# Denominators of the second attention: sums by TensorE in four column quarters of a bank, in place of GpSimd's additions

## The reference

```python
q = (text_hidden @ Wq).reshape(B, T_text, N_HEADS, HEAD_DIM).transpose(0, 2, 1, 3)
k = (vision_tokens @ Wk).reshape(B, T_vis, N_KV_HEADS, HEAD_DIM).transpose(0, 2, 1, 3)
v = (vision_tokens @ Wv).reshape(B, T_vis, N_KV_HEADS, HEAD_DIM).transpose(0, 2, 1, 3)
scores = jnp.einsum('bhtd,bhsd->bhts', q, k) / scale
scores = jnp.where(mask, scores, -jnp.inf)
attn = jax.nn.softmax(scores, axis=-1)
out = jnp.einsum('bhts,bhsd->bhtd', attn, v)
return out.reshape(B, T_text, N_HEADS * HEAD_DIM) @ Wo
```

## Time and profile before

| what | value |
|---|---|
| median of three runs | 1687.81 us (1685.54 to 1689.53) |
| the profiled execution | 1685.9 us, of it the span 1684.5 us |
| mean granted TensorE clock | 0.942 of 2.4 GHz |
| busy, TensorE matmul | 1454.9 us (86%) |
| busy, VectorE | 1229.2 us (73%) |
| busy, ScalarE | 1127.1 us (67%) |
| busy, GpSimd | 792.1 us (47%) |
| chain that ended last | PE L582 35%, POOL L1878 6%, DVE L1514 3% |

### The profile page before, as it was taken

One profiled execution on the slowest core, in us unless ns is written; L12 is line 12 of the kernel. 1 busy time (PEld: TensorE's weight loads), 2 busy tenths in 40 slices (PEclk: granted clock), 3 DMA queues, 4 the chain that ended last, 5 costly groups with the idle time before them and its releaser, 6 DMA issues.

```text
span 1684.5 us, 25330 instructions
## 1 busy us (share of the span) xinstructions
PE 1454.9 (86%) x8374; PEld 711.7 (42%) x8460; DVE 1229.2 (73%) x2184; ACT 1127.1 (67%) x2020; POOL 792.1 (47%) x615
## 2 busy tenths in 40 slices
PE   5687988888888887688898989899899999999979
PEld 3243343343333343244444444344544455455445
DVE  6765766666686356478887768899589997788937
ACT  3567667667764755477787668678477775788724
POOL 3014013014030001078766749787486877577823
PEclk8798997897999999799999999999999999999989
DMA  4001200200340100100000100000000000000000
GB/s 154 1 1 39 43 1 11 50 1 1 60 176 1 51 1 5 39 21 6 1 1 23 38 20 6 26 1 1 6 26 1 26 1 1 1 1 1 1 1 26
DMA packets 20488, 36.69 MB, mean 22 GB/s; under 512 B 4898, under 2 KB 15238, under 8 KB 19334
## 3 DMA queue, kind: packets, MB, share of 16 engines
q1 hardware_dynamic: 20358, 35.07, 7.2%
HBM read 26.53 MB, written 1.15 MB: 16 GB/s over the span
## 4 chain that ended last, share of the span: by engine, by line
PE 35%; POOL 9%; issue 7%; DVE 5%; ACT 3%; POOLq 0%; DMA 0%; ACTq 0%; DVEq 0%; SPq 0%
PE BK L582 35%; POOL arena L1878 6%; DVE arena L1514 3%; DVE arena L1497 1%; ACT arena L1760 1%; ACT arena L1768 1%; POOL arena L1875 1%; POOL arena L1853 1%; ACT arena L1753 1%; POOL arena L1884 1%; POOL arena L1863 1%; DVE arena L886 0%; PE BK L866 0%; ACT L1753 0%; DVE arena L1528 0%
## 5 line engine op out<-in xcount | busy, mean ns | idle before, releaser
L582 PE MATMUL BK<-arena 128*128 128x512 bf16 (+10 forms) x8044 | 1407.2, 378 | 192.6 <-DVE arena L1497 30.6
L582 PEld LDWEIGHTS BK<-arena 128*128 128x128 bf16 (+7 forms) x8130 | 674.2, 115 | 894.8 <-issue 235.1
L1878 POOL TENSOR_TENSOR arena<-arena 128x512 f32<-128x512 f32 (+1 forms) x352 | 509.5, 1447 | 178.6 <-ACT arena L1753 154.5
L1514 DVE TENSOR_TENSOR arena<-arena 128x512 bf16<-128x512 f32 (+1 forms) x416 | 514.4, 1245 | 39.7 <-ACT arena L1760 38.8
L1753 ACT ACTIVATE arena<-BK,arena 128x512 f32<-128x512 f32 (+1 forms) x416 | 285.9, 687 | 132.3 <-PE BK L582 117.1
L1329 DVE TENSOR_REDUCE arena<-BK 128x1 f32<-128x512 f32 x384 | 244.0, 683 | 65.6 <-PE BK L582 64.4
L1661 ACT ACTIVATE arena<-BK 128x512 f32<-128x512 f32 (+1 forms) x416 | 226.0, 598 | 76.0 <-PE BK L582 69.6
L1760 ACT CAST arena<-arena 128x512 bf16<-128x512 f32 (+1 forms) x416 | 253.3, 609 | 0.0
L1768 ACT ACTIVATE arena<-BK 128x512 bf16<-128x512 f32 (+1 forms) x256 | 130.0, 508 | 87.8 <-PE BK L582 86.7
L1497 DVE CUSTOM_DVE_ANT_0 arena<-BK,arena 128x512 bf16<-128x512 f32 (+1 forms) x256 | 145.7, 569 | 47.4 <-PE BK L582 37.5
L1802 POOL TENSOR_TENSOR arena<-arena 128x256 f32<-128x256 f32 (+6 forms) x45 | 30.2, 671 | 208.1 <-ACT arena L1600 205.7
(11 more groups left out here) (170 smaller groups left out, 863.8 us busy)
## 6 DMA issues: line engine op xcount, KB each, us to landing
arena<-arena SPq DMA_DIRECT2D x144, 50.0 KB, 2.2
arena<-in_ctxT SPq DMA_DIRECT2D x8, 800.5 KB, 4.4
arena<-in_ctxk SPq DMA_DIRECT2D x4, 768.0 KB
arena<-in_wo SPq DMA_DIRECT2D x1, 2048.0 KB, 7.9
arena<-in_wqT SPq DMA_DIRECT2D x1, 2048.0 KB, 7.7
arena<-in_x SPq DMA_DIRECT2D x4, 256.0 KB, 11.0
arena<-in_rsel SPq DMA_DIRECT2D x1, 1024.0 KB, 9.2
arena<-in_rw1T SPq DMA_DIRECT2D x1, 1024.0 KB, 5.1
```

The lines of the kernel that those rows point to most:

```text
L582: return T.matmul(out_, lhsT, rhs, start=start, stop=stop, skip_group_check=True)
L1514: V.tensor_tensor(Pl[k][0:m, :], P1[k][0:m, :], Ph[k][0:m, :], ALU.subtract).then_inc(p_low, 1)
L1878: G.tensor_tensor(acc[0:m, g % 2, :], acc[0:m, g % 2, :], P1[k][0:m, :], ALU.add).then_inc(summed1, 1)
```

## The change

GpSimd no longer adds the exponentials. A new piece `su` follows `v1` after each second tile: TensorE sums a pair of tiles over their keys, with 32 columns of bf16 ones (`onb`) as weights. The high and the low halves of the two tiles go to four different column quarters, rows 0, 32, 64 and 96 of bank 6: four products of 512 columns for each pair, seven `su` pieces to a group, the last of them with one tile and so two products, directly behind the sixth. At the end of the group VectorE takes bank 6 to `den` in one pass of 128 x 512 (`o1a`; rows of a quarter are equal, and a lower bound guards against zero). `o1b` multiplies `den` by `quarter`, a matrix with ones in one row of each quarter, so that bank 7 holds the whole denominators on all partitions, and VectorE inverts all 128 x 512 of them into `rc`. ScalarE's copy, VectorE's two small operations, the four products with one column and GpSimd's diagonals are gone.

What comes with it: `P1` is freed by VectorE's `r1` alone; `Ph` and `Pl` get rings of six (`NH`) and are freed by `su`; `finish` begins two steps earlier in the next group (`kt == 3` in place of 5); `qproj` of stage 2 moves from bank 6 to bank 4, which it shares with `md`; GpSimd sets `quarter` and `least` with eight more small memsets in stage 1.

```diff
-LEAD1, LAG1, NR = 6, 3, 4
+LEAD1, LAG1, NR, NH = 6, 3, 4, 6
+L1SET = 11
...
-    def qproj(self, g, bank=6):
+    def qproj(self, g, bank=4):
...
         def finish(g):
-            piece("o1a", g, bank=7)
+            piece("o1a", g)
             yield
             yield
             piece("o1b", g, bank=7)
...
-            if kt == LAG1 + 2 and s > NKT:
+            if kt == LAG1 and NKT < s < ns:
...
-            if kt > LAG1 + 1:
+            if kt >= LAG1:
                 next(og, None)
...
                 piece("v1", s - LAG1)
+                gv, kv = (s - LAG1) // NKT, (s - LAG1) % NKT
+                if kv and kv % 2 == 0:
+                    piece("su", gv, kv // 2 - 1)
+                    if kv == NKT - 1:
+                        piece("su", gv, kv // 2)
...
-                elif kind == "o1a":
-                    g, = arg
-                    pe.wait_ge(summed1, 12 * (g + 1))
-                    pe.wait_ge(l1_set, 4)
-                    for u in range(4):
-                        t = mm(BK[7][:, u:u + 1], acc[:, g % 2, 128 * u:128 * u + 128], ones[:, 0:1])
-                    t.then_inc(full[7], 1)
+                elif kind == "su":
+                    g, u = arg
+                    if u == 0:
+                        pe.wait_ge(den_taken, g)
+                    for kt in range(2 * u, min(2 * u + 2, NKT)):
+                        k, m = (g * NKT + kt) % NH, rows_of(kt)[0]
+                        for n_, part in enumerate((Ph, Pl)):
+                            at = 64 * (kt % 2) + 32 * n_
+                            t = mm(BK[6][at:at + 32, :], onb[0:m, 0:32], part[k][0:m, :], start=(u == 0), stop=(kt >= 11))
+                    t.then_inc(den_summed, 1)
                 elif kind == "o1b":
                     g, = arg
-                    pe.wait_ge(diag_done, g + 1)
-                    mm(BK[7][:, :], ones[:, :], dg[:, :, :].rearrange("p u n -> p (u n)")).then_inc(full[7], 1)
+                    pe.wait_ge(den_taken, g + 1)
+                    mm(BK[7][:, :], quarter[:, :], den[:, :]).then_inc(full[7], 1)
...
                 elif kind == "o1a":
+                    g, = arg
+                    dve.wait_ge(*summed1(NKT * g + NKT - 1))
+                    dve.wait_ge(l1_set, L1SET)
+                    if g:
+                        dve.wait_ge(*filled("o1b", g - 1))
+                    V.tensor_scalar(den[:, :], BK[6][:, :], least[:, 0:1], None, ALU.max).then_inc(den_taken, 1)
+                elif kind == "o1b":
+                    g, = arg
                     dve.wait_ge(full[7], n + 1)
-                    V.tensor_scalar(dn[:, 0:4], BK[7][:, 0:4], 1e-30, None, ALU.max).then_inc(free[7], 1)
-                    dve.wait_ge(free[7], n + 1)
-                    V.reciprocal(dn[:, 4:8], dn[:, 0:4]).then_inc(dn_recip, 1)
+                    dve.wait_ge(pv_taken, g)
+                    V.reciprocal(rc[:, :], BK[7][:, :]).then_inc(free[7], 1)
...
                     act.wait_ge(p_low, s - NR + 1)
-                    if s >= NR:
-                        go, ko = (s - NR) // NKT, (s - NR) % NKT
-                        act.wait_ge(summed1, 12 * go + max(ko, 1))
...
-                elif kind == "o1b":
-                    g, = arg
-                    act.wait_ge(full[7], n + 1)
-                    act.wait_ge(pv_taken, g)
-                    A.copy(rc[:, :], BK[7][:, :]).then_inc(free[7], 1)
...
-                        G.tensor_tensor(acc[:, g % 2, :], P1[(s - 1) % NR][:, :], P1[k][:, :], ALU.add).then_inc(summed1, 1)
...
-                        G.tensor_tensor(acc[0:m, g % 2, :], acc[0:m, g % 2, :], P1[k][0:m, :], ALU.add).then_inc(summed1, 1)
...
-                    G.tensor_tensor(dg[:, :, :], idn[:, :].unsqueeze(1).to_broadcast([128, 4, 128]),
-                                    dn[:, 4:8].unsqueeze(2).to_broadcast([128, 4, 128]), ALU.mult).then_inc(diag_done, 1)
...
```

More of the change, by code:

```diff
@@ L709, in program @@
         on1 = sb("on1", [128, 128], F32, CTb)
-        ones = sb("ones", [128, 128], F32, CTb)
-        dn = sb("dn", [128, 8], F32, CTb)
+        quarter = sb("quarter", [128, 128], F32, CTb)
+        least = sb("least", [128, 1], F32, CTb)
         mng = sb("mng", [4, 2, 128], BF16, CTb)
-        Ph = [sb(f"Ph_{i}", [128, 512], BF16, (L1, CTb)[i == 0]) for i in range(NR)]
-        Pl = [sb(f"Pl_{i}", [128, 512], BF16, (L1, SM)[i == 0]) for i in range(NR)]
+        Ph = [sb(f"Ph_{i}", [128, 512], BF16, (L1, CTb)[i == 0]) for i in range(NH)]
+        Pl = [sb(f"Pl_{i}", [128, 512], BF16, (L1, SM)[i == 0]) for i in range(NH)]
         ckf = sb("ckf", [128, NKT, 128], F32, L1)
@@ L717, in program @@
         mrw = sb("mrw", [128, 2, 512], BF16, SM)
-        acc = sb("acc", [128, 2, 512], F32, L1)
-        dg = sb("dg", [128, 4, 128], F32, SM)
+        den = sb("den", [128, 512], F32, SM)
         rc = sb("rc", [128, 512], F32, L1)
@@ L915, in program, with summed1 @@
         ac_done = sem("ac_done")
[L917 to L920 removed]
+        mcb_done, q_high, max1_done, p_high, p_low, pv_done, den_summed, den_taken, ck_high, ck_low, tern_done = (
+            sem(n) for n in ("mcb_done", "q_high", "max1_done", "p_high", "p_low", "pv_done", "den_summed", "den_taken",
+                             "ck_high", "ck_low", "tern_done"))
+        l1_set, t_gt, t_half, pv_taken = (sem(n) for n in ("l1_set", "t_gt", "t_half", "pv_taken"))
+        def summed1(s):
+            return den_summed, 7 * (s // NKT) + s % NKT // 2 + 1
         def prep_over(queue):
@@ L1756, in scalar_main @@
                     s, = arg
-                    k, m = s % NR, rows_of(s % NKT)[0]
+                    k, m = s % NH, rows_of(s % NKT)[0]
                     act.wait_ge(*emptied("s1", s))
-                    act.wait_ge(pv_done, s - NR + 1)
-                    A.copy(Ph[k][0:m, :], P1[k][0:m, :]).then_inc(p_high, 1)
+                    if s >= NH:
+                        act.wait_ge(*summed1(s - NH))
+                    A.copy(Ph[k][0:m, :], P1[s % NR][0:m, :]).then_inc(p_high, 1)
                 elif kind == "md":
@@ L1894, in gpsimd_main @@
                     G.memset(on1[:, :], 1.0 / (1024 * 256)).then_inc(l1_set, 1)
-                    G.memset(ones[:, :], 1.0).then_inc(l1_set, 1)
                     G.memset(onb[:, :], 1.0).then_inc(l1_set, 1)
                     G.memset(mrw[:, :, :], 0.0).then_inc(l1_set, 1)
+                    G.memset(quarter[:, :], 0.0).then_inc(l1_set, 1)
+                    G.memset(least[:, :], 1e-30).then_inc(l1_set, 1)
+                    pool.wait_ge(l1_set, 5)
+                    for q in range(4):
+                        G.memset(quarter[32 * q:32 * q + 1, :], 1.0).then_inc(l1_set, 1)
+                    for q in (1, 3):
+                        G.memset(least[32 * q:32 * q + 32, :], -3e38).then_inc(l1_set, 1)
                 elif kind == "meet":
```

34 lines of the change are left out of this document (7 added, 27 removed).

## The result

The changed kernel takes **1761.17 us** (median of four runs, 1754.99 to 1766.18) against 1688.67 for the kernel before in the same comparison. The ratio is 1.0434, with a 95% interval of 1.0412 to 1.0456: 72.5 us slower, 4.3%. The forecast was 1763. The profiled execution is the longest of the four, 1766.2 us with a span of 1764.9, so it lies 80.3 us over the one of before.

What follows compares the result with a forecast made beforehand. TensorE was taken to set the pace in full groups of the second attention. 62 + 57 + 2 - 45 = +76 us on the profiled 1685.9 gives 1762, for the median 1763 us; range 1703 to 1792.

Steps and rivals of the forecast that it cites:

- sums on TensorE: Second attention: `su` costs 2.74 us a group, less 0.81 for products removed: net 1.93 us, 32 times, +62 us.
- stall of the inversion: End of each group: TensorE idles 1.9 us in 29 groups and 1.2 in two, until `ql` is done: +57 us.
- the end: Last group's denominators to `o1c`: 6.0 us and 0.3 for the last sums, against 4.3 before: +2 us.
- relief: Groups that are not full: VectorE and ScalarE, freed of GpSimd's additions, win back part of 78 us: -45, bounds 20 to 70.
- What bounds the kernel: Second attention: TensorE, busy 23.92 of a full group's 24.25 us, sets the pace; relief elsewhere can win 78 us at most.
- Gives nothing: Full groups of the second attention: whatever is taken from GpSimd there wins no time, as TensorE alone sets the pace.
- rival of whole drains: At `su`: each change of shape costs the whole 0.16 us, 23 us more, 1786 us; chance 0.05.
- The straight line: VectorE's inversion: three rows up to 64 columns lie on one line, so 512 columns take 3.3 us.
- stalls add up: Rival: background pieces behind the inversion lengthen its stall, with falls of the clock: 1783 to 1798 us; chance 0.09.
- the forecast's case: Whole kernel: the forecast of 1763 us, its own case spanning 1740 to 1785 (relief 70 to 20); chance 0.61.
- groups with masks shorter by over 8 us: Second attention, groups with masks: a sign that would show the forecast wrong, the relief being undersized.
- At nothing: Parts costed at zero: `den`'s pass, the first `su`'s wait, rings of six, eight memsets in stage 1, DMA.

Runs made afterwards that it cites:

- run 2: The changed kernel with a plain copy of bank 7 in place of the inversion: 1697.81 us, ratio to the kernel before 1.0047.
- run 1: The kernel before with eleven of GpSimd's twelve additions a group left out, nothing in their place: 1636.36 us, ratio 0.9686.
- run 5: The changed kernel with twelve GpSimd additions a group, constants into a scratch tile nobody reads: 1797.31 us, ratio to the kernel before 1.0644.
- runs 2 and 3: Run 2 has its own line; 3 is the changed kernel with the inversion in four pieces of 128 columns, a step apart: 1704.05 us, ratio 1.0092.

## Why the prediction was right

The total came within 2 us, and the mechanism is as forecast: slots on TensorE, and a stall behind the inversion. But the terms are off by up to 8 us, and two of them hide parts that the prediction did not have:

| term | forecast | measured | from |
|---|---|---|---|
| sums on TensorE | +62 | +62 | distances between starts; busy time of full groups |
| stall of the inversion | +57 | +63 | run 2 |
| the end | +2 | +1 | last group |
| relief | -45 | -53 (-46 to -60) | run 1 |
| all | +76 | +73 | +72.5 in medians, +80.3 between the profiled executions |

- **What bounds the kernel.** Right: run 1 takes only 0.19 us off a full group. "Gives nothing" was a little too strong, and this is a part of why a full group came to 27.57 us and not to 28.1: 24.25 + 1.95 (sums) + 1.73 (stall) would be 27.93, and the changed kernel is 0.36 below that, of which the 0.19 explain about half. The rest is open.
- **Sums on TensorE.** 0.31 and 0.33 us as read from two other stages, four quarters at once; 2.76 us a group against 2.74. The rival of whole drains (12 x 0.06 us more a group) is out. The Trainium skill (TensorEngine Tiling (Array Packing), Key Properties) calls a change of tiling mode a drain; here it costs 0.09 us on the way in and 0.11 on the way out, less than the 0.16 us by which a result trails its slot.
- **The inversion.** 3358 ns against 3.3 us. The straight line through 4, 32 and 64 columns held over a factor of eight: from 948 ns for 128 columns to 3358 for 512 it is 6.3 ns a column.
- **The stall.** The mechanism, the engines and the releaser (`ql`, in 28 gaps) are as forecast. The gap in full groups is 1.73 us against 1.9, since VectorE's operations overlap by some 0.08 us each: `r1` starts at 1577.11, before the inversion's record ends at 1577.20. What its removal gives, 63 us, is near the 57 in part by luck. The prediction counted the plain gap alone. Background pieces add some 14 us to the gaps ("stalls add up" was a rival with a chance of its own, and is a part of the forecast's case), the lower clock that came with the waits adds up to 20 in the profiled execution, and the gap behind the relu, which appears once the inversion is gone, takes back about as much.
- **The relief.** The term that was mis-sized most: -53 against -45, within its bounds of 20 and 70. Its cause was also thinner than it should have been: the prediction named the ring, the waits and VectorE's time together, and run 5 speaks for VectorE's speed beside GpSimd as the larger part. Its sign of an undersized relief, groups with masks shorter by over 8 us, did not come: in run 1 no group is shorter by more than 6.1.
- **At nothing.** `den`'s pass waited 1.5 us in all on its 32 occasions (L1533), all of it in the last group, and TensorE shows no gap at `su`. No second stall stands behind the inversion in full groups of the changed kernel. The one that runs 2 and 3 show, with 0.77 us, is on ScalarE, to which the prediction gave no part in a stall.
- **The end.** The prediction took `o1b` at 2.04 us, read where the granted clock was 0.57; in the changed kernel it took 1.10 at 0.84, so the end grew by 1.1 us and not by 2.
- **Its arithmetic.** The sums come out, but for the span of the forecast's own case: a relief of 70 to 20 us gives 1738 to 1788 and not 1740 to 1785.

The two terms that err (6 us too little, 8 too much) cancel; the total is better than its parts deserve.

## What to carry to other kernels

Price one long operation on an in-order queue by what stands behind it and is waited for, not by the engine's share: VectorE went from 73% to 64% busy, and TensorE waits for it more than before. Where such an operation is needed, cut it into pieces with the urgent work between them; that gave back 57 of 63 us here without computing less. Moving work onto the engine that sets the pace is paid in full, so what it relieves must be worth more than its slots: here 53 us of relief stood against 62 of slots even before the stall.

Gains of single repairs don't add. Once a stall is gone, ask which engine is the next to be late (here ScalarE's relu, then a norm behind `o1p`): what is saved ahead of that wait is lost in it.

## What was unexpected in the hardware's numbers

- VectorE's `r1` took 722 ns on average with GpSimd silent, 1029 with twelve additions a group that share no data with it, and some 1200 in the full groups of the kernel before. Twelve such additions a group, on which nobody waits, cost the changed kernel 36 us.
- A stall costs more than its idle time where the granted clock falls with it. A group with the same 133 products has 25.86 us of busy time at a granted clock of 1.00 and 27.45 at 0.94, and it was the run with the longer gaps that had more such groups.
- Records of four products in four column quarters start nearly together and cost one slot (0.22 us), whether there are two or four of them: 76.4 against 78.4 us of busy time for 384 and 768.
- Four inversions of 128 columns cost 13% more VectorE time than one of 512 (3.8 against 3.36 us), a small fixed part for an operation of that length.
